# Two attention passes interleaved pair by pair, and key tiles transposed in a score bank

## The chip, the cores and the metric

The kernel runs on one core of one Trainium2 chip. The metric is the device time of one execution in microseconds (us); the median of three runs stands against the median of the changed kernel. Engines are named as the profile names them: PE is TensorE's matmul stream and PEld its weight loads, DVE is VectorE, ACT is ScalarE, POOL is GpSimd, SP is the engine that issues most DMAs.

## The reference, cut to what matters

A perceiver block: cross attention of 256 latent rows on 4096 context rows, then a random-feature attention, then a mixture of experts. The change touches only the first.

```python
xn = layernorm(x, ln_x_g, ln_x_b)              # 4096 context rows of 256
ln = layernorm(latents, ln_l_g, ln_l_b)        # 256 latent rows
q = (ln @ Wq).reshape(b, m, h, d).transpose(0, 2, 1, 3)   # 16 heads of 64
kv = jnp.concatenate([xn @ Wkv, ln @ Wkv], axis=1)
qn = rmsnorm(q, qn_g) * scale
kn = rmsnorm(k, kn_g)
sim = jnp.einsum('bhid,bhjd->bhij', qn, kn)
attn = softmax(sim)
out = einsum(attn, v)                          # then out @ Wout + bout
```

(In the kernel, x of this block is the context and the latents are the model's 256 rows; both kinds of rows are keys, so there are 4352 of them.)

## The kernel before, in words

**Tiles, units, passes.** The 4352 key rows are 34 tiles of 128 rows (`NT`), taken two at a time as 17 units (`NU`). The 16 heads are done in 4 passes (`NPASS`) of 4 heads. A step n is one tile in one pass, so there are 136 steps; the program is written in pairs m of two steps, 68 in all, 17 of each pass. Steps run pass by pass: pair 0 to 16 is pass 0, 17 to 33 is pass 1, and so on.

**Preparing a unit**, once, in pass 0: VectorE takes row statistics (`statistics`, L618 and L625), GpSimd the root (`root_of`, L810 and L815), ScalarE and VectorE subtract the mean and scale a tile each (`center`, L482 and L639), TensorE transposes four 128x128 blocks (`transpose_z`, L345) into a PSUM bank, ScalarE applies the gain (`gain`, L491) and rounds to fp32r (L495), VectorE keeps the rounding rest (`rest`, L645) in `xn`. Products of fp32 numbers are taken as three fp32r products of first parts and rests.

**A step**: TensorE projects a tile on keys and values (`project`, L168, 6 matmuls of 512 columns into `kv_ps`); ScalarE squares the keys (`square`, L516) and keeps the values (`keep_v`, L523); VectorE sums (`mean_square`, L689), GpSimd takes the root (`root`, L796), VectorE scales (`scale_k`, L667, tile `kn`); TensorE transposes (`transpose_k`, L372), ScalarE and VectorE split the result (`keep_kt`, L530, and `kt_rest`, L693); TensorE takes the scores (`scores`, L386, two banks for each parity of n); ScalarE takes the exponents (`weights`, L538), VectorE adds them up (`add_weights`, L683), TensorE weights the values (`weight_v`, L399, into `o_ps` of the pass's parity).

**Order.** Each engine runs its own hand-written loop over m, in order, and waits on semaphores. In pair m with e = 2m, TensorE does project(e+2), project(e+3), transpose_k(e), transpose_k(e+1), the query work if it is due, transpose_z(m+3), weight_v(e-2), weight_v(e-1), scores(e), scores(e+1). ScalarE does weights(e-2), weights(e-1), square(e+2), keep_kt(e), keep_kt(e+1), keep_v(e+2), square(e+3), keep_v(e+3), gain(m+3), center(m+4). VectorE does add_weights of e-2 and e-1, with rest(m+2) behind the first, mean_square(e+2), kt_rest(e), kt_rest(e+1), statistics(m+4), the last add_weights, scale_k(e+2), mean_square(e+3), center(m+4), scale_k(e+3). `project(n)` waits for kn and v of step n-2, since `kv_ps` has two banks.

**Between passes.** Queries of pass t are made over five pairs around `query_pair(t, 0)`: `queries_hi` on ScalarE (L501), `queries_lo` on GpSimd (L819), `project_q` on TensorE, `square_q`, `mean_square_q` (L649), `root_q` (L823), `scale_q` (L653), `transpose_q`, and at stage 2 `keep_qt` (ScalarE L510) and `qt_rest` (VectorE L659). The pass's weights are split by `weights_hi` (ScalarE L548) and `weights_lo` (GpSimd L801, one instruction of 1024 columns). For pass 1 stage 0 is pair 14 and the weights fall in pairs 11 and 12.

Of the kernel before, what the change touches and what calls it, by code (L numbers as in the profile page):

```python
# [178 lines left out]
def attention(nc, sem, a, x_res, ident, ones, neg_half, fw, ew):  # L179
# [4 lines left out]

    V_RING = 6
    P_RING = 4
    with ExitStack() as ctx:
# [58 lines left out]

        def exists(n):
            return 0 <= n < STEPS

# [3 lines left out]
        def zt_ps(k):  # L253

            return o_ps[1][:, k, :]
# [9 lines left out]
        def ended(m):  # L265

            g = (m + 1) // NU - 1
            return g if 0 <= g < NPASS and (g + 1) * NU - 1 == m else None

        def query_pair(t, stage):  # L270

            return (NU - 3 if t == 1 else (t - 1) * NU + 9) + stage

        @block.sync
        def _(sp):
# [18 lines left out]
            sp.dma_start(bout[:], a["L0_xattn_bout"].partition_broadcast(P)).then_inc(bout_in, 16)  # L294
            for g in range(4, NG + 1):
# [17 lines left out]
            for g in range(1, NPASS):  # L313
                sp.wait_ge(wq_lo, g)
                load_queries(g)
                sp.wait_ge(w_lo, g)
                load_weights(g)
                if g >= 2:
                    sp.wait_ge(y_done, g - 1)
                    load_wout(g - 1)  # L320
# [4 lines left out]
        def _(pe):  # L325
            def project(n):
                g, t, b = n // NT, n % NT, n % 2
                if t == 0:
                    pe.wait_ge(w_lo, g + 1)
# [18 lines left out]
            def project_q(t):  # L348
                if t == 0:
                    pe.wait_ge(xn_lo, 1)  # L350
                elif t == 1:
                    pe.wait_ge(affine_done, NU)
                else:
                    pe.wait_ge(y_added, t - 1)
# [20 lines left out]
            def scores(n):  # L375
                g, b = n // NT, n % 2
                pe.wait_ge(kt_lo, n - n % 2 + 2)
                if n % NT == 0:
                    pe.wait_ge(qt_lo, g + 1)
                if n >= 2:  # L380
                    pe.wait_ge(exp_done, 2 * (n - 1))
                for j in range(2):
                    for t, (s, m) in enumerate(((0, 0), (0, 1), (1, 0))):
                        for c in range(2):
                            half = slice(c * DH, (c + 1) * DH)
                            last = nc.tensor.matmul(s_ps[b][c][:, j, :], kt[b][half, s, j * P:(j + 1) * P],  # L386
                                                    q_parts[g % 2][half, j, m, :], start=t == 0, stop=t == 2)
                            if j == 1 and t == 2:
                                last.then_inc(s_done, 1)

            def weight_v(n):
                g, t = n // NT, n % NT
# [11 lines left out]
            def totals(g):  # L404
                pe.wait_ge(sum_done, 2 * (g + 1) * NT)
# [24 lines left out]
            for m in range(STEPS // 2 + 1):  # L430
# [14 lines left out]
                if m + 3 < NU:  # L445
                    transpose_z(m + 3)
# [18 lines left out]
        def _(act):  # L465
# [53 lines left out]
            def keep_v(n):  # L519
                if n >= V_RING:  # L520
                    act.wait_ge(pv_done, n - V_RING + 1)
                t = n % NT
# [17 lines left out]
            def keep_sums(g):  # L540
                act.wait_ge(pv_done, (g + 1) * NT)
# [27 lines left out]
            for m in range(STEPS // 2 + 1):  # L569
# [18 lines left out]
                if m + 3 < NU:  # L588
# [904 lines left out]
```

## Time and profile before

| | us |
|---|---|
| median of three runs | 704.05 (703.61 to 705.65) |
| time of the profiled execution | 703.4 |
| its span in the trace | 701.7 |
| PE busy in the span | 660.5 (94%) |
| DVE busy | 499.3 (71%) |
| ACT busy | 417.2 (59%) |
| POOL busy | 236.7 (34%) |

The attention takes the trace from the start to about 540 us, of which 36.2 to 540 is the regular loop. Busy time of PE holds overlaps of one matmul with the next, so the length of a pair is best read from the distance between two starts of the same work, for which `weight_v` (L399) is taken below.

### The profile page before, as it was taken

What the parts mean: (1) busy time and instruction counts of PE and PEld (TensorE: products, weight loads), DVE (VectorE), ACT (ScalarE), POOL (GpSimd) and SP (SyncE); (2) the same over time, 40 slices, a digit from 0 to 9 for tenths busy, and PEclk for the clock granted to TensorE, in tenths of its full rate; (3) what the DMA queues carried; (4) which work ended last, traced back from release to release, by engine and by line L of the source; (5) the groups of instructions that cost most, each with busy time, mean ns of one, the idle gap of its engine ahead of it and who ended that gap; (6) DMA issues with size and microseconds to landing.
All of it is one profiled execution on the core that took longest, in us unless ns stands there. A gap on an engine that the chain in (4) does not pass through costs nothing. (4 is left out here: it accounts for less than half of the span.)

```text
span 701.7 us, 14395 instructions
## 1 busy us (share of the span) xinstructions
PE 660.5 (94%) x5152; PEld 526.8 (75%) x5152; DVE 499.3 (71%) x977; ACT 417.2 (59%) x878; POOL 236.7 (34%) x219
## 2 busy tenths in 40 slices
PE   1899999899999999999999999999998997899997
PEld 0777776677677777777777777777776886899997
DVE  2798898866867677687768767767676636867573
ACT  3687888656556666665666666566663313565650
POOL 3544434532233242222334332232220023355640
PEclk9999999999999999999999999999999989999999
DMA  5111460100000000000000000000002104256500
GB/s 161 36 56 32 123 182 1 46 1 2 1 16 16 2 31 1 2 1 16 1 2 1 1 2 1 16 2 1 1 2 68 53 1 164 78 196 218 166 19 16
DMA packets 26131, 30.50 MB, mean 43 GB/s; under 512 B 4169, under 2 KB 23762, under 8 KB 26066
## 3 DMA queue, kind: packets, MB, share of 16 engines
q1 hardware_dynamic: 23410, 28.79, 12.9%
q10 hardware_dynamic: 2656, 0.86, 0.5%
q8 instruction: 39, 0.64, 0.4%
q14 instruction: 26, 0.21, 0.1%
HBM read 29.38 MB, written 0.26 MB: 42 GB/s over the span
## 5 line engine op out<-in xcount | busy, mean ns | idle before, releaser
L796 POOL TENSOR_TENSOR k_rms<-k_ss,neg_half 128x4 f32<-128x4 f32 x136 | 137.1, 1008 | 312.6 <-DVE k_ss L689 312.6
L538 ACT ACTIVATE probs<-s_ps,minus_bound 128x512 f32<-128x512 f32 x272 | 164.6, 688 | 90.2 <-PE s_ps L386 90.2
L168 PE MATMUL kv_ps<-w_quad,xn 128*128 128x512 f32 x816 | 211.0, 405 | 1.6 <-issue 1.5
L683 DVE SCALAR_TENSOR_TENSOR probs_sum<-probs,tile_mask,probs_sum 128x512 f32<-128x512 f32 x264 | 192.4, 765 | 5.2 <-ACT probs L538 4.8
L168 PEld LDWEIGHTS kv_ps<-w_quad,xn 128*128 128x128 f32 x816 | 147.3, 188 | 45.0 <-issue 6.4
L399 PE MATMUL o_ps<-probs,v 128*64 128x256 f32 x1088 | 132.6, 385 | 0.8 <-ACT probs L538 0.7
L386 PEld LDWEIGHTS s_ps<-q_parts,kt 64*128 64x128 f32 x1632 | 101.1, 185 | 36.0 <-issue 19.6
L386 PE MATMUL s_ps<-q_parts,kt 64*128 64x256 f32 x1632 | 114.9, 287 | 9.2 <-DVE kt L693 9.2
L667 DVE SCALAR_TENSOR_TENSOR kn<-k_rms,kv_ps 128x256 f32<-128x256 f32 x136 | 56.7, 417 | 67.5 <-POOL k_rms L796 67.0
L399 PEld LDWEIGHTS o_ps<-probs,v 128*64 128x64 f32 x1088 | 72.0, 136 | 41.9 <-issue 10.7
L530 ACT ACTIVATE kt<-s_ps 128x256 fp32r<-128x256 f32 x136 | 44.9, 383 | 63.9 <-PE s_ps L372 63.6
L693 DVE TENSOR_TENSOR kt<-s_ps,kt 128x256 fp32r<-128x256 f32 x136 | 51.0, 416 | 33.0 <-ACT kt L530 33.0
L523 ACT ACTIVATE v<-kv_ps,tile_mask 128x256 f32<-128x256 f32 x136 | 66.4, 488 | 0.0
L689 DVE TENSOR_REDUCE k_ss<-k_sq 128x4 f32<-128x256 f32 x136 | 55.9, 411 | 1.8 <-ACT k_sq L516 1.7
L516 ACT ACTIVATE k_sq<-kv_ps 128x256 f32<-128x256 f32 x136 | 54.2, 399 | 1.8 <-PE kv_ps L168 1.8
L372 PE MATMUL s_ps<-ident,kn 128*128 128x128 f32 x272 | 41.2, 273 | 0.6 <-ACT probs L538 0.6
L372 PEld LDWEIGHTS s_ps<-ident,kn 128*128 128x128 f32 x272 | 33.7, 140 | 10.4 <-issue 1.0
L1392 DVE CAST e_act_p<-e_act_f 128x1024 fp32r<-128x1024 f32 x18 | 17.7, 985 | 26.3 <-PE e_y_ps L1300 25.6
L1348 ACT ACTIVATE e_act_f<-e_h_ps,e_b_now 128x256 f32<-128x256 f32 x72 | 27.7, 486 | 5.6 <-DVE e_act_p L1394 3.5
L1246 POOL TENSOR_TENSOR w_first<-w_raw,w_first 128x2048 fp32r<-128x2048 f32 x4 | 21.6, 5402 | 23.5 <-ACT w_first L1332 23.5
L1246 POOL TENSOR_TENSOR e_w_second<-w_raw,e_w_second 128x2048 fp32r<-128x2048 f32 x4 | 21.5, 5364 | 23.6 <-ACT e_w_second L1332 19.6
L168 PE MATMUL e_h_ps<-e_zp,w_first 128*128 128x256 f32 x240 | 29.0, 280 | 0.4 <-DVE e_zp L1416 0.4
(185 smaller groups left out, 666.7 us busy)
## 6 DMA issues: line engine op xcount, KB each, us to landing
w_raw<-in_ffn_W SPq DMA_DIRECT2D x18, 1024.0 KB, 5.2
rows<-in_ctx SPq DMA_DIRECT2D x8, 512.0 KB, 3.9
w_raw<-in_L_xattn_Wkv SPq DMA_DIRECT2D x6, 256.0 KB, 3.1
wout<-in_L_xattn_Wout SPq DMA_DIRECT2D x4, 256.0 KB, 2.7
wq_raw<-in_L_xattn_Wq SPq DMA_DIRECT2D x3, 256.0 KB, 3.3
w_raw<-in_L_xattn_Wkv ACTq DMA_DIRECT2D x2, 256.0 KB, 6.7
x_res<-in_x SPq DMA_DIRECT2D x1, 256.0 KB, 3.6
wq_raw<-in_L_xattn_Wq ACTq DMA_DIRECT2D x1, 256.0 KB, 4.1
```

The source lines that it names most:

```text
L168: last = nc.tensor.matmul(out, stationary(k, s), moving(k, m), start=n == 0, stop=n == len(terms) - 1)
L372: last = nc.tensor.transpose(kt_ps(n)[:, j * P:(j + 1) * P], kn[n % 2][:, j].rearrange("p c d -> p (c d)"), ident[:])
L386: last = nc.tensor.matmul(s_ps[b][c][:, j, :], kt[b][half, s, j * P:(j + 1) * P], q_parts[g % 2][half, j, m, :], start=t == 0, stop=t == 2)
L399: last = nc.tensor.matmul(o_ps[g % 2][c * DH:(c + 1) * DH, j, :], v[n % V_RING][:, j, c, :], probs[n % P_RING][:, j, c, :], start=t == 0 a ...
L516: nc.scalar.activation(k_sq[n % 2][:].rearrange("p j c d -> p (j c d)"), kv_ps[n % 2][:, 0, :], ACT.Square, scale=DH ** -0.5).then_inc(sq_ ...
L523: nc.scalar.activation(v[n % V_RING][:].rearrange("p j c d -> p (j c d)"), kv_ps[n % 2][:, 1, :], ACT.Copy, scale=tile_mask[:, t:t + 1]).t ...
L538: nc.scalar.activation(probs[n % P_RING][:, :, c, :], s_ps[n % 2][c][:], ACT.Exp, bias=minus_bound[:]).then_inc(exp_done, 1)
L667: nc.vector.scalar_tensor_tensor(kn[n % 2][:], k_rms[n % 2][:].unsqueeze(3).to_broadcast([P, 2, 2, DH]), 1.0 / RMS_FLOOR, kv_ps[n % 2][:, ...
L683: nc.vector.scalar_tensor_tensor(total, probs[n % P_RING][:, :, c, :], seen, total, ALU.mult, ALU.add).then_inc(sum_done, 1)
L689: nc.vector.reduce_sum(k_ss[n % 2][:], k_sq[n % 2][:], AX_X).then_inc(ss_done, 1)
L693: nc.vector.tensor_tensor(kt[n % 2][:, 1, :], kt_ps(n), kt[n % 2][:, 0, :].bitcast(F32), ALU.subtract).then_inc(kt_lo, 1)
L796: nc.gpsimd.tensor_tensor(k_rms[n % 2][:].rearrange("p i c -> p (i c)"), k_ss[n % 2][:].rearrange("p i c -> p (i c)"), neg_half[:, 0:4], A ...
```

## The change

The order of pairs is now a list, `plan`: four pairs of pass 0, then one of pass 1 before every two of pass 0, until pass 0 is through (plan positions 4, 7, 10, 13, 16, 19 and 22 are pass 1), then the rest of pass 1, and passes 2 and 3 as before. Pass 0 ends at position 23, pass 1 at 33. `unit_of` gives the pair in which a unit is transposed: pairs 0, 2, 3, 5, 6, 8, 9, 11, 12, 14, 15, 17, 18 and 20 for units 3 to 16; its statistics and center stand one pair ahead, its rest one pair behind. Since both `o_ps` banks are in use, a unit is transposed in `s_ps[1][0]`, a score bank: the transposes wait for the exponents of step e-1, half 0, and scores(e+1) waits for `gain`. `gain` moves ahead of keep_v(e+2). Pass 1's queries and weights are now due at the very start (stage 0 is pair 2, `weights_hi` pair 0, `weights_lo` pairs 1 and 2), those of pass 2 at pairs 31 and 26 to 28. `weights_lo` is two instructions of 512 columns, a pair apart.

```diff
+        ahead, plan = 4, []
+        for u in range(NU):
+            if u >= ahead and (u - ahead) % 2 == 0:
+                plan.append((1, (u - ahead) // 2))
+            plan.append((0, u))
+        taken = sum(g for g, _ in plan)
+        plan += [(1, u) for u in range(taken, NU)] + [(g, u) for g in range(2, NPASS) for u in range(NU)]
+        place = {step: m for m, step in enumerate(plan)}
+        unit_of = {place[0, u] - 3: u for u in range(3, NU)}
...
-            return o_ps[1][:, k, :]
+            return s_ps[1][0][:, k, :]
...
-            return (NU - 3 if t == 1 else (t - 1) * NU + 9) + stage
+            return (2, 2 * NU - 3, 2 * NU + 9)[t - 1] + stage
+        def weights_pair(g):
+            return (0, place[0, NU - 1] + 3, 2 * NU + 11)[g - 1]
...
+                if u >= 4:
+                    pe.wait_ge(exp_done, 2 * (2 * (place[0, u] - 3) - 1) + 1)
...
+                if b and n // 2 in unit_of:
+                    pe.wait_ge(affine_done, unit_of[n // 2] + 1)
...
-                if m + 3 < NU:
-                    transpose_z(m + 3)
+                if m in unit_of:
+                    transpose_z(unit_of[m])
...
+                if m in unit_of:
+                    gain(unit_of[m])
                 if exists(e + 2):
                     keep_v(e + 2)
                     square(e + 3)
                     keep_v(e + 3)
-                if m + 3 < NU:
-                    gain(m + 3)
...
-                    if m == query_pair(t, -3):
+                    if m == query_pair(t, -2):
                         queries_hi(t)
...
+                if m - 1 in unit_of:
+                    rest(unit_of[m - 1])
...
-                    if m == query_pair(t, -2):
+                    if m == query_pair(t, -1):
                         queries_lo(t)
...
-                if m % NU == NU - 5 and m // NU < NPASS - 1:
-                    weights_lo(m // NU + 1)
+                    for k in range(KD):
+                        if m == weights_pair(t) + 1 + k:
+                            weights_lo(t, k)
```

VectorE, from the scaled keys at the end of pair 2 to the key parts of pair 3. `q_ss` and `qn` are the query work, `xn` is rest(4) here and rest(5) before, `kt` the key parts for which the scores of pair 3 wait. Before:

```order
L667 SCALAR_TENSOR_TENSOR kn<-k_rms,kv_ps 128x256
L779 TENSOR_TENSOR x_res<-x_res,bout 128x512
L683 SCALAR_TENSOR_TENSOR probs_sum<-probs,tile_mask,probs_sum 128x2x256
L645 TENSOR_TENSOR xn<-affine,xn 128x2x2x128
L683 SCALAR_TENSOR_TENSOR probs_sum<-probs,tile_mask,probs_sum 128x2x256 x2
L689 TENSOR_REDUCE k_ss<-k_sq 128x4
L693 TENSOR_TENSOR kt<-s_ps,kt 128x256 x2
```

and after:

```order
L696 SCALAR_TENSOR_TENSOR kn<-k_rms,kv_ps 128x256
L678 TENSOR_REDUCE q_ss<-q_sq 128x8
L810 TENSOR_TENSOR x_res<-x_res,bout 128x512
L682 SCALAR_TENSOR_TENSOR qn<-q_rms,o_ps 128x512
L712 SCALAR_TENSOR_TENSOR probs_sum<-probs,tile_mask,probs_sum 128x2x256
L674 TENSOR_TENSOR xn<-affine,xn 128x2x2x128
L712 SCALAR_TENSOR_TENSOR probs_sum<-probs,tile_mask,probs_sum 128x2x256 x2
L718 TENSOR_REDUCE k_ss<-k_sq 128x4
L722 TENSOR_TENSOR kt<-s_ps,kt 128x256 x2
```

Two query instructions now stand between the scaled keys and the first sum of exponents.

GpSimd, after the changed loop has begun, pairs 1 and 2 (`wq`, `w_quad` are pass 1's query and key-value weights, `q_rms` its queries' root); before, pairs 1 and 2 hold only the two roots and the unit's root:

```order
L850 TENSOR_TENSOR wq<-wq_raw,wq 128x2x256
L832 TENSOR_TENSOR w_quad<-w_raw,w_quad 128x512
L827 TENSOR_TENSOR k_rms<-k_ss,neg_half 128x4
L841 TENSOR_SCALAR var_eps<-mean_var 128x2
L846 TENSOR_TENSOR rstd<-var_eps,neg_half 128x2
L827 TENSOR_TENSOR k_rms<-k_ss,neg_half 128x4
L854 TENSOR_TENSOR q_rms<-q_ss,neg_half 128x8
L832 TENSOR_TENSOR w_quad<-w_raw,w_quad 128x512
```

ScalarE in pair 0, from the key parts to the first exponents. Before:

```order
L530 ACTIVATE kt<-s_ps 128x256 x2
L523 ACTIVATE v<-kv_ps,tile_mask 128x256
L516 ACTIVATE k_sq<-kv_ps 128x256
L523 ACTIVATE v<-kv_ps,tile_mask 128x256
L491 ACTIVATE affine<-o_ps,gains 128x256 x2
L495 ACTIVATE xn<-affine 128x2x2x128
L482 ACTIVATE z<-rows,mean_off,rstd 128x256
L538 ACTIVATE probs<-s_ps,minus_bound 128x2x256 x4
```

and after:

```order
L559 ACTIVATE kt<-s_ps 128x256 x2
L520 ACTIVATE affine<-s_ps,gains 128x256 x2
L524 ACTIVATE xn<-affine 128x2x2x128
L552 ACTIVATE v<-kv_ps,tile_mask 128x256
L545 ACTIVATE k_sq<-kv_ps 128x256
L552 ACTIVATE v<-kv_ps,tile_mask 128x256
L530 ACTIVATE wq<-wq_raw 128x2x256
L577 ACTIVATE w_quad<-w_raw 128x2x512
L567 ACTIVATE probs<-s_ps,minus_bound 128x2x256 x4
```

The gain moved ahead of the kept values and the square, and the weights' first parts stand where the center of the next unit stood.

## Rows read from the trace of the kernel before

**Rows 1.** Page, the span in 40 slices: busy tenths of PE

```profile
PE   1899999899999999999999999999998997899997
```

**Rows 2.** Windows from weight_v to weight_v: stretch, length, busy PE, PEld, DVE, ACT, POOL

```profile
213.61:220.56 6.95, 6.95 (x57) 5.22 (x56) 5.50 (x10) 4.36 (x11) 2.66 (x3) 1.00 0.11 37
220.56:228.91 8.35, 8.35 (x69) 6.67 (x68) 5.92 (x13) 5.78 (x15) 3.03 (x3) 1.00 0.01 2
36.23:43.61 7.38, 7.38 (x62) 5.66 (x61) 6.59 (x17) 6.40 (x16) 3.33 (x4) 1.00 0.03 10
50.97:59.05 8.08, 7.64 (x61) 5.58 (x61) 7.30 (x18) 6.40 (x16) 3.33 (x4) 1.00 0.00 1
59.05:66.61 7.56, 7.56 (x61) 5.56 (x60) 6.77 (x18) 6.39 (x15) 3.33 (x4) 1.00 0.23 63
111.99:119.96 7.97, 7.80 (x61) 5.49 (x60) 5.72 (x17) 6.80 (x14) 3.33 (x4) 1.00 0.00 0
119.96:128.60 8.64, 7.71 (x62) 5.57 (x61) 7.86 (x17) 7.35 (x19) 6.33 (x6) 1.00 0.04 8
128.60:139.02 10.42, 8.42 (x70) 6.67 (x69) 9.29 (x18) 6.88 (x17) 3.71 (x4) 1.00 0.22 71
153.31:161.23 7.92, 7.00 (x58) 5.22 (x57) 6.80 (x14) 4.36 (x11) 2.02 (x2) 1.00 0.00 0
```

**Rows 3.** Timeline of a pair with a unit: start, length, engine, line, work

```profile
83.62 1.69 PE L386 MATMUL s_ps<-q_parts,kt 64*128 64x256 f32 x24
...
86.35 0.42 DVE L667 SCALAR_TENSOR_TENSOR kn<-k_rms,kv_ps 128x256 f32<-128x256 f32 x1 [0.50 <-POOL k_rms L796]
...
86.84 1.23 PEld L168 LDWEIGHTS kv_ps<-w_quad,xn 128*128 128x128 f32 x6 [0.37 <-issue]
```

**Rows 4.** Timeline of a pair without a unit, pass 1

```profile
215.48 1.71 PE L386 MATMUL s_ps<-q_parts,kt 64*128 64x256 f32 x24
...
217.10 0.42 DVE L667 SCALAR_TENSOR_TENSOR kn<-k_rms,kv_ps 128x256 f32<-128x256 f32 x1 [1.12 <-POOL k_rms L796]
```

**Rows 5.** Timeline: sums and rests of VectorE beside GpSimd's weight rests

```profile
126.80 2.83 POOL L801 TENSOR_TENSOR w_quad<-w_raw,w_quad 128x1024 fp32r<-128x1024 f32 x1
...
127.32 2.85 DVE L645 TENSOR_TENSOR xn<-affine,xn 128x512 fp32r<-128x512 f32 x1
...
132.54 1.69 PE L386 MATMUL s_ps<-q_parts,kt 64*128 64x256 f32 x24 [2.00 <-DVE kt L693]
...
248.80 2.07 DVE L683 SCALAR_TENSOR_TENSOR probs_sum<-probs,tile_mask,probs_sum 128x512 f32<-128x512 f32 x3
...
254.96 3.87 DVE L683 SCALAR_TENSOR_TENSOR probs_sum<-probs,tile_mask,probs_sum 128x512 f32<-128x512 f32 x3
```

**Rows 6.** Timeline of pairs 0 and 1: ScalarE's gain and exponents, second projection

```profile
30.56 1.05 ACT L491 ACTIVATE affine<-o_ps,gains 128x256 f32<-128x256 f32 x2
...
31.64 0.63 ACT L495 ACTIVATE xn<-affine 128x512 fp32r<-128x512 f32 x1
...
33.27 0.42 DVE L667 SCALAR_TENSOR_TENSOR kn<-k_rms,kv_ps 128x256 f32<-128x256 f32 x1 [0.49 <-POOL k_rms L796]
...
33.79 1.64 PE L168 MATMUL kv_ps<-w_quad,xn 128*128 128x512 f32 x6 [0.24 <-issue]
```

**Rows 7.** Timeline of pass 2's query work: scores, sum, scaled queries, scores two pairs later

```profile
230.79 1.69 PE L386 MATMUL s_ps<-q_parts,kt 64*128 64x256 f32 x24
231.34 0.68 DVE L649 TENSOR_REDUCE q_ss<-q_sq 128x8 f32<-128x512 f32 x1
...
233.77 0.69 DVE L653 SCALAR_TENSOR_TENSOR qn<-q_rms,o_ps 128x512 f32<-128x512 f32 x1 [1.75 <-POOL q_rms L823]
...
246.07 1.70 PE L386 MATMUL s_ps<-q_parts,kt 64*128 64x256 f32 x24 [0.92 <-DVE kt L693]
```

**Rows 8.** One line each: GpSimd's query weight rest, VectorE's rest, min/median/max ns

```profile
L819 POOL TENSOR_TENSOR wq<-wq_raw,wq x4: 1282/1296/1449, 16.4 to 341.7; 128x512 fp32r<-128x512 f32 x4
L645 DVE TENSOR_TENSOR xn<-affine,xn x17: 677/685/2855, 15.9 to 135.9; 128x512 fp32r<-128x512 f32 x17
```

More of the change, by code:

```diff
@@ L245, in attention, with step, last_step @@
         block = ctx.enter_context(nc.Block())
+        ahead, plan = 4, []
[7 more added lines that the diff above has]
+        unit_of = {place[0, u] - 3: u for u in range(3, NU)}
         def exists(n):
             return 0 <= n < STEPS
+        def step(n):
+            g, u = plan[n // 2]
+            return g, 2 * u + n % 2
+        def last_step(g):
+            return 2 * place[g, NU - 1] + 1
         def source(u):
@@ L312, in _ @@
                 sp.dma_start(fw.proj_bd[DHP * h:DHP * (h + 1), h, :], a["L0_attn_proj"]).then_inc(fw.proj_in, 16)
-            for g in range(1, NPASS):
+            for g in range(2, NPASS):
                 sp.wait_ge(wq_lo, g)
                 load_queries(g)
-                sp.wait_ge(w_lo, g)
+                sp.wait_ge(w_lo, KD * g)
                 load_weights(g)
-                if g >= 2:
-                    sp.wait_ge(y_done, g - 1)
-                    load_wout(g - 1)
+                sp.wait_ge(y_done, g - 1)
+                load_wout(g - 1)
             sp.wait_ge(y_done, NPASS - 1)
@@ L326, in project @@
             def project(n):
-                g, t, b = n // NT, n % NT, n % 2
+                (g, t), b = step(n), n % 2
                 if t == 0:
-                    pe.wait_ge(w_lo, g + 1)
+                    pe.wait_ge(w_lo, KD * (g + 1))
                 if g == 0:
@@ L375, in scores @@
             def scores(n):
-                g, b = n // NT, n % 2
+                (g, t), b = step(n), n % 2
                 pe.wait_ge(kt_lo, n - n % 2 + 2)
-                if n % NT == 0:
+                if t == 0:
                     pe.wait_ge(qt_lo, g + 1)
@@ L386, in scores @@
                             last = nc.tensor.matmul(s_ps[b][c][:, j, :], kt[b][half, s, j * P:(j + 1) * P],
-                                                    q_parts[g % 2][half, j, m, :], start=t == 0, stop=t == 2)
-                            if j == 1 and t == 2:
+                                                    q_parts[g % 2][half, j, m, :], start=term == 0, stop=term == 2)
+                            if j == 1 and term == 2:
                                 last.then_inc(s_done, 1)
             def weight_v(n):
-                g, t = n // NT, n % NT
+                g, t = step(n)
                 if t == 0:
@@ L596, in _ @@
                         square_q(t)
-                if m % NU == NU - 6 and m // NU < NPASS - 1:
-                    weights_hi(m // NU + 1)
+                    if m == weights_pair(t):
+                        weights_hi(t)
             keep_sums(NPASS - 1)
@@ L671, in add_weights @@
             def add_weights(n, c):
-                g, t = n // NT, n % NT
+                g, t = step(n)
                 dve.wait_ge(exp_done, 2 * n + 1 + c)
@@ L749, in _ @@
                     add_weights(e - 2, 0)
-                if m + 2 < NU:
-                    rest(m + 2)
+                if m == 0:
+                    rest(2)
+                if m - 1 in unit_of:
+                    rest(unit_of[m - 1])
                 if exists(e - 2):
@@ L759, in _ @@
                         kt_rest(n)
-                if m + 4 < NU:
-                    statistics(m + 4)
+                if m + 1 in unit_of:
+                    statistics(unit_of[m + 1])
                 if exists(e - 2):
@@ L832, in _ @@
             root_of(1)
-            weights_lo(0)
+            for k in range(KD):
+                weights_lo(0, k)
             queries_lo(0)
@@ L856, in _ @@
                         root_q(t)
-                if m % NU == NU - 5 and m // NU < NPASS - 1:
-                    weights_lo(m // NU + 1)
+                    for k in range(KD):
+                        if m == weights_pair(t) + 1 + k:
+                            weights_lo(t, k)
                 if m == 10:
```

39 lines of the change are left out of this document (21 added, 18 removed).

## The prediction
> **What bounds the kernel now.** I read the page's slices first: from the second slice to the end of the attention PE stands at 9 tenths and at 8 in one slice [rows 1]. A busy PE hides waits of some tenths, so next come windows cut from one weight_v to the next. A pair of pass 1 takes 6.95 us, the first row of [rows 2]; PE is the limit there, since almost all pairs of three passes have that length. The same pair with a query projection takes 8.35, so that work is 1.40. The second pair of pass 0, with a unit, takes 7.38 (36.23 to 43.61), so the four transposes of a unit cost 0.43 of TensorE. Any length beyond 6.95, plus 0.43 with a unit, plus 1.40 with queries, is a wait. The change gives TensorE the same matmuls in another order, so the only thing that can move is the sum of these waits, in the first 24 to 36 pairs.
>
> **The waits of before that the change touches** [rows 2]:
> - Seven ordinary pairs of pass 0 between 59 and 112 us have 7.56, not 7.38: 0.18 each, 1.3 in all. The cause is in the timeline: with a unit, the second scaled key (kn) starts 2.73 us after the scores of its pair begin (86.35 against 83.62) and the second projection of the next pair starts only behind it, at 3.22, with 0.37 idle in front [rows 3]; without a unit kn starts at 1.62 (217.10 against 215.48) [rows 4] and nothing waits. The chain behind a unit is 1.1 us longer, and its slack was some 0.9.
> - 8.08 at 50.97: the same with an addition of `bout` on VectorE, 0.7.
> - 7.97, 8.64 and 10.42 at 112 to 139, where pass 1's weights and queries are made beside units: 0.59 + 1.26 + (10.42 - 6.95 - 1.40 =) 2.07 = 3.9. The largest part is one row: rest (L645), 0.68 as a rule [rows 8], took 2.85 while GpSimd took its weight rest, and the scores then waited 2.00 for kt [rows 5].
> - 7.92 at 153.31, stage 2 of pass 1's queries: 0.97.
> In all 1.3 + 0.7 + 3.9 + 1.0 = **6.9 us** of waits. All of it is gone or moved; TensorE's own work is not less. That is the most that the change could give.
>
> **What comes in their place.** The query and weight work of pass 1 now lies in pairs 0 to 4, which also prepare units, with an empty pipeline behind them. S(m) is the start of the scores of pair m.
> - *Pair 0.* ScalarE's gain (1.05 + 0.63 [rows 6]) now stands ahead of the second square, which comes about 2.0 later. VectorE and GpSimd hid part of that: kn of step 3 goes from 33.27 to about 34.0, and the projection behind it from 33.79 to 34.5: **0.7**.
> - *Pair 1.* Statistics without transposes: kn ends about 3.3 after S(1), where TensorE could project at about 3.0: **0.35**. Behind it GpSimd takes wq and the first half of w_quad, 1.3 each (the 512 columns of [rows 8]).
> - *Pair 2.* The two GpSimd rests run while VectorE wants to add exponents. What that costs is in the trace: three sums took 2.07 alone and 3.87 while GpSimd took 1024 columns [rows 5]. I take 1.3 to 2 us; it uses up most of the 1.40 that the query projection gives the other engines. What is left of it is a late kn, **0.3**. That VectorE is less ahead is what matters next.
> - *Pair 3.* In pass 2 the scaled queries (qn) start 2.98 after the scores (233.77 against 230.79), the sum before them at 0.55 [rows 7]. Here kn is 2.6 later against the scores (a unit with its statistics 1.1, GpSimd's rests about 1.5), so q_ss begins near 3.2 and qn, 2.43 behind it as in [rows 7], near 5.6; it ends at 6.3. TensorE's transpose_q, due at 5.0, waits **1.2** for it. Then VectorE has still to do, before kt: one sum that waits out the second w_quad half on GpSimd (0.6), three sums (2.0), rest 0.6, k_ss 0.35 and kt 0.75, which ends near 10.6. The scores could start at 9.1. A further **1.6**.
> - *Pair 4.* Stage 2: `qt_rest` waits for ScalarE behind the exponents, which cost 0.92 in pass 2 [rows 7]; here rest(5) (0.6) stands in the same row, ahead of kt: **1.6**.
> - *Pair 5.* VectorE has no slack left from pair 4, and statistics follow at once. kn is 0.7 later than in an ordinary unit pair: 0.18 + 0.7, **0.85**.
> In all 6.6 us; the same counted over the whole stretch from S(0) to S(5) gave 6.4, which I take.
> - *Later units, pairs 6 to 20.* Where transposes and statistics fall in one pair (8, 11, 14, 17), VectorE has no rest to take there and is 0.6 earlier: no wait. In pairs with transposes alone kn ends about 2.7 after the scores, 0.3 before TensorE wants it: none. In pairs with statistics alone (7, 10, 13, 16, 19) TensorE lacks the 0.43 of cover, and kn is 0.1 later than in [rows 3]: 0.3 each, **1.5**.
> - *The new waits.* Scores(e+1) waits for the gain. Behind the transposes TensorE has weight_v, 1.87 (213.61 in [rows 2] to 215.48 in [rows 4]), and scores(e), half of 1.69; the gain needs 1.05 [rows 6] of these 2.7, so it costs nothing, and 1.6 us of lateness of ScalarE are covered. The transposes wait for the third of four exponents, and weight_v right behind them needs the second and the fourth anyway: nothing.
> - *The rest.* Prologue 0.2 (GpSimd's two halves are 2.6 where one was 2.4, and VectorE's rest waits for them); the first half of pass 2's weights beside the normalisation of pass 0, 0.1. Loads of pass 1 are issued from 16 us on and needed from 33: hidden. Query stages of passes 2 and 3 stay as they are.
> Sum: 6.4 + 1.5 + 0.3 = 8.2 of waits for 6.9, **1.3 us more**. The profiled execution would go from 703.4 to 704.7; the median of before lies 0.65 above its profiled execution, so the forecast is 704.05 + 1.3 = **705.3**. Against the early chain stands no row of the same place, so I bound it: if GpSimd's rests fit in gaps and qn is as early as in [rows 7], pairs 0 to 5 cost 2.5, and the whole comes to 4.3 - 6.9 = -2.6; if each step adds, 9 us and +3.9.
>
> A rule beside this. The rows show a VectorE instruction with both inputs in SBUF lengthened by as much as GpSimd's overlaps it (2.85 for 0.68, 3.87 for 2.07) [rows 5]. The Trainium skill, in "SBUF — State Buffer", section "Who interferes with whom", says that such an instruction and a GpSimd instruction that reads SBUF exclude each other, and that the one issued later is blocked for the whole instruction. By that rule the `bout` addition in pair 2 also holds back GpSimd's root of the queries, by up to 0.6, and the sum would be 1.9 and the time 705.9; I left it out, as no row shows a root held back by it.
>
> **Rivals.**
> - *Faster: the early pairs are absorbed.* For: VectorE has 1.1 to 1.4 idle in a pair without a unit, and two of pairs 0 to 5 have none to transpose; in pass 2 the query stages 0 and 1 cost nothing. Against: the 3.87 row and that rest and queries meet in pairs 3 and 4. Pairs 0 to 5 at 2.5 and the statistics pairs at 0 to 1.5: 704.05 - 2.6 to -4.1, about **700.7**. Chance 0.2.
> - *Slower: gain ahead of keep_v makes ScalarE's chain the limit in every unit pair.* The second square of a pair comes 1.68 later; VectorE's sum of squares is 0.6 later in a pair with transposes alone than in [rows 4], and kn has 0.9 to spare there. It decides once the lateness passes 0.9. At 0.3 beyond that, in 14 unit pairs, 4.2 more: 704.05 + 1.3 + 4.2 = **709.5**. Chance 0.12.
> - *Slower: the early chain at its upper bound*, 9 us for pairs 0 to 5: 704.05 + 3.9 = **708**. Chance 0.16.
> - *The plan does not do what it says*: the even spread brings no pair under 7.38, since TensorE was the limit. This is no case of its own; it is what the sum rests on.
>
> **How the numbers follow.** Forecast case 0.52, at 705.3, itself 703.5 to 707. About 0.3% is what a measurement of this kernel can tell from no change: 702.0 to 706.1. The forecast case lies mostly within (0.43), a little above (0.09); the faster rival lies below 702 with 0.17 and within with 0.03; both slower rivals are above, 0.28. So faster 0.17, the same 0.46, slower 0.37. The range takes the forecast, most of the faster rival and the upper bound of the early chain: 701.0 to 708.5.
>
> **What would show it.** From weight_v to weight_v: 6.95 for plain pairs, 7.38 for pairs with transposes from pair 6 on, 7.2 to 7.3 in pairs behind statistics alone; the 10.42 gone; two long pairs at plan positions 3 and 4 with kt as what the scores wait for; a DVE rest and sums lengthened beside w_quad at 41 to 54 us. Wrong would be: waits of the scores for `affine` (ScalarE) on PE, waits in each unit pair, or a first stretch to pair 5 that is no more than 3 us longer than TensorE's work.

## The result, and the profile after

| | before | after |
|---|---|---|
| time, median of 7 runs each | 704.06 us (703.27 to 705.86) | 707.75 us (706.92 to 708.18) |
| profiled execution | 703.4 us | 706.92 us |
| its span | 701.7 us | 705.1 us |
| first to last weight_v (windows) | 491.13 us | 495.90 us |

The changed kernel is slower: the ratio is 1.0046, with an interval of 1.0036 to 1.0056. That is 3.7 us where +1.3 was forecast, and above the bound of 0.3%. The likeliest case had been "the same"; the time lies inside the range.

The page of after, first its busy times, then TensorE's two rows of slices:

```profile
PE 660.0 (94%) x5152; PEld 526.9 (75%) x5152; DVE 498.5 (71%) x977; ACT 418.5 (59%) x878; POOL 238.4 (34%) x223
...
PE   1878999999999999999999999999998998899997
...
PEclk9998999999999999999999999999999999999999
```

Against [rows 1] the third and fourth slice of PE (35.3 to 70.5 us) have fallen from 9 to 7 and 8, and the eighth (123 to 141 us), where the pair of 10.42 us was, has risen from 8 to 9. In the fourth slice the granted clock is lower too.

The same windows as in [rows 2], from weight_v to weight_v (stretch, length, busy PE, PEld, DVE, ACT, POOL, granted clock, DMA share, GB/s). The window of pair m begins with the weight_v of pair m and holds the scores of pair m and then the projections and transposes of pair m+1; the first five are pairs 1 to 5 of the plan, the last two are later ones:

```profile
36.63:45.84 9.21, 9.03 (x73) 7.00 (x72) 8.42 (x18) 5.59 (x14) 6.28 (x6) 1.00 0.19 57
45.84:60.88 15.04, 9.99 (x65) 7.72 (x65) 9.66 (x23) 7.09 (x15) 7.58 (x7) 0.77 0.00 1
60.88:67.81 6.93, 6.93 (x57) 5.21 (x56) 2.94 (x7) 6.04 (x13) 1.01 (x1) 1.00 0.00 0
67.81:77.65 9.84, 7.71 (x61) 5.58 (x61) 8.78 (x22) 5.29 (x13) 3.36 (x5) 1.00 0.15 51
77.65:85.00 7.35, 7.35 (x61) 5.64 (x60) 6.62 (x17) 6.49 (x15) 3.33 (x4) 1.00 0.02 7
...
91.92:99.54 7.62, 7.58 (x61) 5.57 (x60) 6.83 (x19) 5.28 (x13) 3.34 (x5) 1.00 0.23 62
99.54:106.91 7.37, 7.37 (x61) 5.66 (x60) 6.66 (x17) 6.50 (x15) 3.34 (x4) 1.00 0.03 10
```

The count of matmuls tells what is in a window: 57 is a plain pair (6.95), 61 holds four transposes as well (+0.43), 65 holds eight (+0.86), 73 holds a query projection and four transposes (+1.83). What is beyond that is waiting: 9.21 - 8.78 = 0.43; 15.04 - 7.81 = **7.23**; 6.93 nothing; 9.84 - 7.38 = 2.46; then nothing. One window stands out, 45.84 to 60.88, and its clock (0.77) says that part of its excess is no wait at all. It is the window of pair 2; what the prediction counts as its pair 3, from the scores of pair 2 to those of pair 3, lies in it and in the start of the next.

The timeline of that window, with two rows of pair 0 ahead of it and one of pair 4 behind it (start, length, engine, line, work, and in brackets the idle time before it and what ended it):

```profile
30.66 1.69 PE L415 MATMUL s_ps<-q_parts,kt 64*128 64x256 f32 x24 [0.61 <-DVE kt L722]
...
34.62 1.64 PE L168 MATMUL kv_ps<-w_quad,xn 128*128 128x512 f32 x6 [0.23 <-issue]
...
47.72 1.68 PE L415 MATMUL s_ps<-q_parts,kt 64*128 64x256 f32 x24
...
50.39 0.68 DVE L678 TENSOR_REDUCE q_ss<-q_sq 128x8 f32<-128x512 f32 x1
...
50.99 0.68 DVE L810 TENSOR_TENSOR x_res<-x_res,bout 128x512 f32<-128x512 f32 x1
...
51.15 2.01 POOL L854 TENSOR_TENSOR q_rms<-q_ss,neg_half 128x8 f32<-128x8 f32 x1 [1.13 <-DVE q_ss L678]
...
53.13 1.26 POOL L832 TENSOR_TENSOR w_quad<-w_raw,w_quad 128x512 fp32r<-128x512 f32 x1
...
54.45 5.19 PE L168 MATMUL kv_ps<-w_quad,xn 128*128 128x512 f32 x12 [5.05 <-POOL w_quad L832]
...
64.38 3.07 PE L168 MATMUL kv_ps<-w_quad,xn 128*128 128x512 f32 x12
...
71.27 1.69 PE L415 MATMUL s_ps<-q_parts,kt 64*128 64x256 f32 x24 [1.51 <-DVE kt L722]
```

After the scores of pair 2 (47.72) TensorE is to project for pair 4 of the plan, the first of pass 1. That projection is the first to read pass 1's `w_quad`, and the second half of this tile is the last work of GpSimd's own pair 2. GpSimd's sequence at that point is q_rms, then the weight rest; q_rms waits for `q_ss`, the sum that VectorE gets to at 50.39. So the rest lands at 54.39, and TensorE, whose scores ended at 49.40, has stood for 5.05 us. Then it pays again: its clock fell during the wait, and the two projections take 5.19 where the same 12 matmuls take 3.07 in the next pair. The window over those first matmuls gives the clock (0.50, the 1.2 GHz level); the trace has it at that level from 52.34 to 59.17:

```profile
54.45:57.00 2.55, 2.55 (x6) 2.07 (x7) 2.42 (x4) 0.00 (x0) 0.00 (x0) 0.50 0.02 6
```

Of the view of TensorE's waits over the span, the two lines that bear on the loop:

```profile
PE s_ps L415 <- DVE kt L722: 7.5, 10, 1.5
...
PE kv_ps L168 <- POOL w_quad L832: 5.0, 1, 5.0
```

The whole loop (first to last weight_v) and the stretch behind it up to the first transposes of the expert stage, of before and then of after:

```profile
36.23:527.36 491.13, 480.17 (x3869) 360.95 (x3869) 370.20 (x773) 324.06 (x729) 166.15 (x169) 1.00 0.07 19
527.36:585.12 57.76, 53.98 (x295) 44.86 (x295) 30.83 (x54) 16.01 (x19) 7.22 (x6) 0.94 0.13 40
```

```profile
36.63:532.53 495.90, 481.89 (x3873) 363.25 (x3872) 371.50 (x781) 325.12 (x730) 168.51 (x174) 0.99 0.06 18
532.53:588.71 56.18, 52.40 (x294) 43.27 (x295) 30.82 (x54) 16.02 (x19) 7.16 (x6) 0.97 0.13 40
```

The loop is 4.8 us longer. The stretch behind it is 1.6 shorter, with code that the change does not touch: TensorE's clock stood at 1.2 GHz for 3.41 us there, where it had been 6.83 us before. The prologue adds 0.4 (the first scores begin at 30.66 for 30.26), pair 0 costs another 0.43, and the first weight_v comes only 0.4 later all the same, because the four transposes of unit 4 (0.43) have moved behind it. So 4.8 + 0.4 stands at the last weight_v, and 4.8 + 0.4 - 1.6, with 0.2 less in the last stage, is the 3.4 us between the spans. So the loop's window is the measure for everything below; totals carry 1.6 us or more that come and go with the clock of the later stages. (The stretches at the lower clock are taken from the trace's own clock records; a window gives their sum, as (1 - 0.97) of 56.18, twice, is 3.4.)

### The profile page after: what moved, and what is told of

Read it like the earlier page. It is cut to its first block and busy times, and to the rows that moved or that the text cites. A ratio compares the mean times of both kernels' runs of the same rounds, so it can differ in the third digit from the quotient of the medians.

```text
span 705.1 us, 14413 instructions
## 1 busy us (share of the span) xinstructions
PE 660.0 (94%) x5152; PEld 526.9 (75%) x5152; DVE 498.5 (71%) x977; ACT 418.5 (59%) x878; POOL 238.4 (34%) x223
## 5 line engine op out<-in xcount | busy, mean ns | idle before, releaser
L168 PEld LDWEIGHTS kv_ps<-w_quad,xn 128*128 128x128 f32 x816 | 149.1, 190 | 50.2 <-issue 5.8
L1279 POOL TENSOR_TENSOR e_w_second<-w_raw,e_w_second 128x2048 fp32r<-128x2048 f32 x4 | 21.4, 5362 | 23.5 <-ACT e_w_second L1365 19.6
```

Of the source, the lines that this page charges most:

```text
L168: last = nc.tensor.matmul(out, stationary(k, s), moving(k, m), start=n == 0, stop=n == len(terms) - 1)
```

## The experiments

Three questions were open: how much of the loss is the wait for the weights (e1, e2); whether the unit's new place or order costs anything alone (e4); and whether the interleave has a gain of its own, or whether its parts in the old order do the same (e3, e5, e6, e7, e8, e9). Ratios are times against the kernel before.

### e1: both weight halves in one pair

```diff
-                        if m == weights_pair(t) + 1 + k:
+                        if m == weights_pair(t) + 1 + (k if t > 1 else 0):
                             weights_lo(t, k)
```

> Edit on the changed kernel: both halves of pass 1's w_quad rest run on GpSimd in pair 1, none in pair 2 behind the queries' root. Theory (first projection of pass 1 waits for the second half, 5.05 us, and TensorE's clock falls to its lower level behind that wait, which costs another 2.2): the wait for w_quad and the low clock are gone; in their place come the waits for the scaled queries and for kt that the prediction counted, 2 to 3 us in pair 3. Attention 7.2 - 2.8 = 4.4 us shorter, total 703 to 704. Rival (the wait only hides an equally late chain on VectorE): pair 3 still takes over 13 us, total 707 or more.

Measured: 705.4 us, ratio 1.0017 (1.0006 to 1.0027). Its loop, and the window that was 15.04:

```profile
37.59:529.37 491.78, 480.31 (x3873) 361.57 (x3872) 371.97 (x781) 324.94 (x730) 168.92 (x174) 1.00 0.06 19
```

```profile
46.82:57.02 10.20, 8.34 (x66) 6.00 (x65) 7.82 (x19) 6.87 (x15) 5.55 (x6) 1.00 0.00 0
```

What is left to wait for there, from its timeline:

```profile
50.57 1.64 PE L168 MATMUL kv_ps<-w_quad,xn 128*128 128x512 f32 x6 [0.19 <-issue]
...
52.51 1.67 PE L168 MATMUL kv_ps<-w_quad,xn 128*128 128x512 f32 x6 [0.29 <-DVE kn L696]
...
53.13 2.01 POOL L854 TENSOR_TENSOR q_rms<-q_ss,neg_half 128x8 f32<-128x8 f32 x1 [1.13 <-DVE q_ss L678]
...
55.99 0.66 PE L389 MATMUL o_ps<-ident,qn 128*128 128x128 f32 x4 [1.38 <-DVE qn L682]
...
59.57 1.69 PE L415 MATMUL s_ps<-q_parts,kt 64*128 64x256 f32 x24 [0.61 <-DVE kt L722]
```

The window is 4.84 shorter, 0.67 comes back in the next one (7.60 for 6.93), and the loop is 4.1 shorter, as expected. The loop is now 0.65 above that of before. With the weights out of the way TensorE waits for a late kn (the projections start late and with a gap, about 0.8 together by the distances between starts), then for qn (1.38 idle, 1.5 by the starts), and then for kt (0.61 idle, 0.65 in the next window): those are the three waits that the prediction had put here. The edit also takes the second half's hold on VectorE out of this pair, so it does not leave the rest exactly as in the changed kernel. The total came out 1.4 above the 704 of the expectation. Its profiled execution shows where: by the trace's clock records TensorE's clock rose at 24.36 us instead of 21.62, so its first projections took 4.46 instead of 3.20 and the loop began 1 us later (ahead of these records the clock row reads 1.00, but the 12 matmuls of the query projection take 2.90 there in both traces and 1.66 in the loop), and the stretch behind the loop was back at 57.78.

### e2: something for TensorE to do while it waits

Twenty matmuls of the identity are run ahead of the wait for the weight half. They leave the real work as it is; nothing reads what they write. The profile shows each as two records (x40).

```diff
             def project(n):
                 (g, t), b = step(n), n % 2
+                if t == 0 and g == 1:
+                    pe.wait_ge(kn_done, n - 1)
+                    pe.wait_ge(v_kept, n - 1)
+                    keep_busy(nc, kv_ps[b][:, 0, 0:P], ident[:], ident[:], 20)
```

> Edit on the changed kernel: 20 matmuls of the identity (results are never read) stand on TensorE ahead of the wait for w_quad, so that the wait stays but TensorE is busy in most of it. Theory: the granted clock stays at its upper level from 52 to 59 us, the two projections behind the wait take 3.1 us in place of 5.2, pair 3 goes from 15.0 to about 12.8, and the total falls by about 2 us unless later stages give it back. Rival (the 5.2 us of these projections have another cause, such as reads of w_quad beside GpSimd): pair 3 stays at 15.0 and the time stays at 707.7.

Measured: 706.46 us, ratio 1.0031 (1.0018 to 1.0044). Its loop, and the window:

```profile
36.78:530.66 493.88, 484.48 (x3913) 366.19 (x3912) 371.54 (x781) 325.14 (x730) 168.47 (x174) 1.00 0.06 19
```

```profile
46.02:58.92 12.90, 12.54 (x106) 10.64 (x105) 9.57 (x23) 7.09 (x15) 7.59 (x7) 1.00 0.00 1
```

```profile
49.52 4.73 PE L176 MATMUL kv_ps<-ident 128*128 128x128 f32 x40
...
54.61 3.06 PE L168 MATMUL kv_ps<-w_quad,xn 128*128 128x512 f32 x12 [0.36 <-POOL w_quad L836]
```

The weights come at the same time as in after (the projections start at 54.61 against 54.45), but the clock stays at 1.00 and they take 3.06 instead of 5.19. The window is 2.14 shorter and the loop 2.0. So of the 4.2 us that e1 won, half was the wait and half was the clock that the wait had cost. The total fell only 1.3: behind the loop 1.6 us came back (57.82 against 56.18).

### e4: the unit in a score bank and the gain ahead of keep_v, in the order of before

```diff
-            return o_ps[1][:, k, :]
+            return s_ps[1][0][:, k, :]
...
+                if u >= 4:
+                    pe.wait_ge(exp_done, 2 * (2 * (u - 3) - 1) + 1)
...
+                if b and n // 2 + 3 < NU:
+                    pe.wait_ge(affine_done, n // 2 + 4)
...
+                if m + 3 < NU:
+                    gain(m + 3)
```

(and `gain(m + 3)` taken out where it stood before).

> Edit on the kernel before: only the transposes of units move to the score bank, with their two waits, and gain moves ahead of keep_v; pass order, queries and weights stay. Theory: the new waits and the moved gain cost nothing in unit pairs: 7.56 us a pair or a little less, total 703.5 to 704.5. Rival (gain ahead of keep_v makes ScalarE's chain the limit): 7.8 to 7.9 us in the 14 unit pairs, total 707.5 to 708.5.

Measured: 705.43 us, ratio 1.0019 (1.0010 to 1.0028). The loop, and an ordinary pair with a unit:

```profile
37.66:528.87 491.21, 480.37 (x3870) 360.98 (x3869) 370.31 (x773) 325.26 (x729) 166.13 (x169) 1.00 0.06 19
```

```profile
68.05:75.61 7.56, 7.56 (x61) 5.57 (x60) 6.78 (x18) 6.49 (x15) 3.33 (x4) 1.00 0.03 11
```

The loop is that of before to 0.1 us, and the unit pair is 7.56, as in [rows 2]. The two new waits of TensorE cost nothing in the loop, and ScalarE's earlier gain does not make it late. The rival of 709.5, in which it would, falls. The total missed its expectation by 0.9 at the least (705.43 for 703.5 to 704.5), and what the parts cost lies ahead of the loop, which begins 1.4 later: from the start of pair 0's projections to the first weight_v 11.28 us against 10.48, so 0.8, the price of the gain in pair 0; the other 0.6 is again a clock that rose later (22.99 against 21.54 us, first projections 3.92 against 3.33).

### e5: the old order, pass 1's weights two pairs later

In the kernel before, pass 1's weight rest (pair 12) stands beside the last units and the rest of the query weights. It can be moved out of their way in the order of before too, with two numbers: ScalarE's part to pair 13 and GpSimd's to pair 14.

```diff
-                if m % NU == NU - 6 and m // NU < NPASS - 1:
+                if m in (NU - 4, 2 * NU - 6, 3 * NU - 6):
                     weights_hi(m // NU + 1)
...
-                if m % NU == NU - 5 and m // NU < NPASS - 1:
+                if m in (NU - 3, 2 * NU - 5, 3 * NU - 5):
                     weights_lo(m // NU + 1)
```

> Edit on the kernel before: pass 1's weights are split two pairs later (ScalarE in pair 13, GpSimd in pair 14), behind the last units; no interleaving. Theory (the 3.9 us of waits in pairs 11 to 13 come from queries, weights and units meeting on ScalarE and GpSimd, above all the rest that waited out GpSimd's w_quad): 2.5 to 3.5 us faster, total 700.5 to 701.5. Rival (late weights hold up the start of pass 1, or the scaled queries wait instead): within 1 us of 704.

Measured: 704.02 us (700.0 to 704.84), ratio 0.9979 (0.9962 to 0.9996). The loop, the windows that were 8.64 and 10.42 in [rows 2], and one of the pair two further on:

```profile
36.75:525.88 489.13, 479.88 (x3869) 360.99 (x3869) 369.54 (x773) 323.95 (x729) 165.77 (x169) 1.00 0.07 19
```

```profile
120.11:128.19 8.08, 7.64 (x62) 5.58 (x61) 7.29 (x18) 6.79 (x17) 4.57 (x5) 1.00 0.07 24
128.19:136.53 8.34, 8.34 (x70) 6.66 (x69) 7.21 (x17) 7.72 (x18) 2.78 (x3) 1.00 0.04 12
...
143.90:151.86 7.96, 7.01 (x58) 5.22 (x57) 5.51 (x12) 4.51 (x11) 2.02 (x2) 1.00 0.20 67
```

The 10.42 is now 8.34, where TensorE has no idle time at all, and 8.64 is 8.08. The pair ahead of them is 7.58 for 7.97. One new wait came: the last window has 1.04 more than before (7.96 for 6.92), 0.95 of it idle before the scores, for kt. The three sums that VectorE takes ahead of kt are 3.59 long there, beside GpSimd's weight rest, where they were 2.07 in before. The loop is 2.0 shorter than before and 6.8 shorter than after. The expectation of 2.5 to 3.5 us was missed: 3.0 were gained in three pairs, and 1.0 came back. The median shows less of it (704.02, where before had 704.24 beside it), since its executions lie apart: 700.0 to 700.4 at a granted clock of 0.995, 703.9 to 704.8 at 0.988. The largest of the waits that the interleave spreads is gone without an interleave.

### e3: the halves alone

In the order of before, GpSimd's weight rest is taken in two halves, one in each of two pairs; nothing else is moved.

```diff
-            def weights_lo(g):
+            def weights_lo(g, k):
...
-                if m % NU == NU - 5 and m // NU < NPASS - 1:
-                    weights_lo(m // NU + 1)
+                for k in range(KD):
+                    if m % NU == NU - 5 + k and m // NU < NPASS - 1:
+                        weights_lo(m // NU + 1, k)
```

> Edit on the kernel before: only the w_quad rest in two halves on GpSimd, a pair apart (pairs 12 and 13 for pass 1). Theory: each half shuts out VectorE's two-input work for 1.3 us in place of 2.8 at once; pairs 12 and 13 go from 8.64 and 10.42 to about 8.0 and 9.2, the loop is 1.5 to 2 us shorter, total 702 to 703. Rival (the total of the lock counts, not its length at once): loop as before within 0.5 us.

Measured: 702.19 us, ratio 0.9978 (0.9966 to 0.9990). The loop, the window that was 10.42, and VectorE's rest that had been 2.85 in [rows 5]:

```profile
37.58:527.96 490.38, 480.30 (x3869) 360.98 (x3868) 369.24 (x773) 324.03 (x729) 166.48 (x172) 1.00 0.07 19
```

```profile
129.91:139.26 9.35, 8.43 (x70) 6.68 (x69) 8.23 (x16) 6.89 (x17) 3.28 (x3) 1.00 0.21 71
```

```profile
128.65 1.77 DVE L645 TENSOR_TENSOR xn<-affine,xn 128x512 fp32r<-128x512 f32 x1
```

The rest is held for one half only, 1.77 for 2.85, and the window of the queries gains 1.07 (10.42 to 9.35). The one before it gains nothing (8.64, 8.62), and the one two further on has 0.3 more. The loop gains 0.75, less than the 1.5 to 2 expected: the weight rests are still in the pairs of the last units, and halving them doesn't take them out of there as e5 does. The total is better than the loop by the clock behind the loop (3.4 us at the lower level, 56.15 for 57.76): this ratio must not be read against that of e5.

### e6: both, and `bout` in pair 20

The edits of e3 with ScalarE's part in pair 12 and the halves in pairs 13 and 14, and the addition of `bout` moved:

```diff
-                if m == 2:
+                if m == 20:
```

> Edit on the kernel before: pass 1's weights on ScalarE in pair 12 and their rest in two halves on GpSimd in pairs 13 and 14; the addition of bout moves from pair 2 to pair 20. Theory: of the 6.9 us of waits that the prediction listed, the 0.7 of bout and 2.5 to 3.5 of the 3.9 in pairs 11 to 13 go; from the first to the last weight_v 491.1 becomes 487 to 488, total 700 to 701.5, as far as the low-clock stretches of the later stages do not move. Rival (each delay only moves): loop no shorter than the 489.1 of the run with late weights.

Measured: 703.35 us, ratio 0.9979 (0.9963 to 0.9996). The loop, the pair after 20, and the stretch behind the loop:

```profile
36.81:525.90 489.09, 479.71 (x3869) 361.41 (x3868) 367.99 (x773) 323.31 (x729) 166.05 (x172) 1.00 0.06 19
```

```profile
187.94:198.36 10.42, 8.72 (x65) 6.73 (x64) 7.63 (x16) 4.35 (x11) 3.02 (x3) 1.00 0.01 2
...
525.90:585.31 59.41, 55.64 (x294) 46.39 (x295) 30.84 (x54) 16.01 (x19) 7.15 (x6) 0.91 0.13 38
```

The loop is that of e5. The pair that `bout` left is 7.46 (8.08 before), 0.62 better, but the pair between 187.94 and 198.36 is 10.42 where it had been 9.69: there the normalisation of pass 0's output wants VectorE too, and 0.73 is lost again. The 487 to 488 expected for the loop was missed, and the rival, a loop no shorter than 489.1, held: the wait had only moved. The last row has the lower clock for 10.24 us, and is 1.65 longer than that of before.

### e7: e1, and `bout` in pair 24

```diff
-                if m == 2:
+                if m == 24:
```

(beside the edit of e1).

> Edit on the changed kernel: w_quad's rest wholly in pair 1, and bout's addition moved from pair 2 to pair 24. Theory (the addition held back GpSimd's root of the queries, 2.01 us in place of 1.64): the root takes 1.64 again and pair 3 is 0.3 to 0.4 shorter than the 10.2 without this move. Rival (the root is long because of its own data or the sum before it): root 2.0, pair 3 at 10.2.

Measured: 704.96 us, ratio 1.0010 (0.9999 to 1.0021). The loop, and the window that was 10.20 in e1, with GpSimd's root of the queries in it:

```profile
36.54:527.93 491.39, 480.39 (x3874) 361.60 (x3873) 372.15 (x781) 324.92 (x730) 168.36 (x174) 1.00 0.06 19
```

```profile
45.77:55.52 9.75, 8.33 (x66) 6.00 (x65) 7.21 (x18) 6.87 (x15) 5.17 (x6) 1.00 0.01 2
```

```profile
52.08 1.64 POOL L854 TENSOR_TENSOR q_rms<-q_ss,neg_half 128x8 f32<-128x8 f32 x1 [1.13 <-DVE q_ss L678]
```

The root takes 1.64 without the addition beside it, and 2.01 with it (after and e1), 0.37 more; the window is 0.45 shorter and the loop 0.4.

### e8: the interleave begins four pairs later

If an empty pipeline were the cause of the waits, the same steps some pairs later would be free.

```diff
-        ahead, plan = 4, []
+        ahead, plan = 8, []
...
-            return (2, 2 * NU - 3, 2 * NU + 9)[t - 1] + stage
+            return (6, 2 * NU - 3, 2 * NU + 9)[t - 1] + stage
...
-            return (0, place[0, NU - 1] + 3, 2 * NU + 11)[g - 1]
+            return (4, place[0, NU - 1] + 3, 2 * NU + 11)[g - 1]
```

(with the edit of e1).

> Edit on the changed kernel: pass 1 begins at plan position 8 in place of 4, its queries are made around pair 6 and its weights in pairs 4 and 5 (w_quad's rest wholly in pair 5). Theory (what costs is that queries, weights and units meet, not that the pipeline has just begun): the pairs from weight_v 5 to 9 hold 4.5 to 6 us of waits, as the pairs 1 to 5 do when w_quad is early (0.4 + 2.4 + 0.7 + 2.5), and the loop is 491.5 to 492.5. Rival (the empty pipeline was the cost): under 3 us of waits there, loop 489 to 490.

Measured: 705.58 us, ratio 1.0011 (0.9993 to 1.0028). The loop, and three of the four windows:

```profile
37.59:529.00 491.41, 479.76 (x3869) 361.18 (x3869) 369.86 (x773) 325.10 (x729) 166.85 (x172) 1.00 0.06 18
```

```profile
67.34:76.81 9.47, 9.07 (x73) 7.00 (x72) 8.69 (x17) 5.40 (x13) 7.75 (x7) 1.00 0.17 56
76.81:86.56 9.75, 8.33 (x66) 6.00 (x65) 7.22 (x18) 6.87 (x15) 5.17 (x6) 1.00 0.00 1
...
94.15:103.99 9.84, 7.72 (x62) 5.58 (x61) 8.78 (x22) 5.29 (x13) 3.35 (x5) 1.00 0.17 49
```

Less TensorE's own work these windows wait 0.69, 1.94 and 2.46, and the one between them (7.60, a plain pair) 0.65: 5.7 in all. In e1 the same four wait 0.45 + 2.39 + 0.67 + 2.46 = 6.0 from the second pair of the plan on. The 0.3 between them is `bout`, which no longer stands there. So the empty pipeline is not the cause. What is left is that weights, queries and a unit's statistics want VectorE and GpSimd in the same pairs; e5, which takes the weights out of the units' pairs in the old order, speaks for it, but no run does so in the interleaved one.

### e9: e5, and `bout` in pair 24

```diff
-                if m == 2:
+                if m == 24:
```

(beside the edits of e5).

> Edit on the kernel before: pass 1's weights late (ScalarE in pair 13, GpSimd in pair 14), and bout's addition moved from pair 2 to pair 24, where no unit, query or normalisation stands. Theory (an addition on VectorE costs only where a unit or a normalisation leaves no slack; in pair 20 it cost the next projection out 0.74): pair 3 is 7.5 in place of 8.1, pair 24 stays at 6.95, the loop from first to last weight_v is 488.4 to 488.6. Rival (any added 0.68 us on VectorE is paid somewhere): loop 489.1 as with late weights alone.

Measured: 701.76 us (699.57 to 703.35), ratio 0.9960 (0.9945 to 0.9974). The loop, and the pair that was 8.08:

```profile
37.02:525.59 488.57, 479.72 (x3870) 361.09 (x3869) 369.53 (x773) 323.94 (x729) 165.79 (x169) 1.00 0.06 19
```

```profile
51.74:59.21 7.47, 7.47 (x62) 5.58 (x61) 6.68 (x18) 6.40 (x16) 3.33 (x4) 1.00 0.01 4
```

The loop is 2.6 below that of before, as expected, and the kernel is 2.8 us faster than before and 6.0 faster than the changed one, by its median: three numbers changed in the old order. Executions at the same granted clock say the same: at 0.992 it takes 701.5 to 701.8 where before takes 703.3 to 704.1, at 0.988 703.0 to 703.4 for 705.7 to 706.2.

## Why the prediction was right or wrong

**What bounds the kernel: right.** TensorE was the limit, and the time went by the sum of its waits. The windows less TensorE's own work, known from their matmul counts, account for the change of the loop to 0.1 us (below). One reading was off: in [rows 1] the second slice is an 8 too, so the nines begin at the third; nothing hangs on it.

**Pairs 0, 1, 2: right, but for the split.** Pair 0 was put at 0.7; kn was to go to about 34.0 and came at 34.10, and the projection behind it to 34.5 and came at 34.62. But 0.40 of that lateness was there when pair 0's scores began, so pair 0 itself cost 0.43 and the prologue 0.40 where 0.2 was forecast; together 0.83 for 0.9. In e4, with a unit's statistics and center still in pair 0, the gain costs 0.8. Pair 1 was put at 0.35 and is 0.43. For pair 2 a late kn was put at 0.3; in the changed kernel the wait for the weights covers it, in e1 it is about 0.8.

**Pair 3: the step that failed.** The prediction went from "TensorE's transpose_q, due at 5.0, waits 1.2 for it" to "A further 1.6" for kt, 2.8 in all, 3.1 with pair 2. The windows of pairs 2 and 3 measured 7.23. The "due at 5.0" assumes that TensorE's projections ahead of transpose_q can run. It had the second w_quad half on GpSimd in this very pair, but only as a load on VectorE ("one sum that waits out the second w_quad half on GpSimd"). It did not ask who waits for the half itself: the projection, and it stands ahead of the transposes on TensorE. Nor did it lay out GpSimd's queue, in which the half stands behind q_rms, and q_rms behind a VectorE sum. e1 takes this wait away, and with it the half's hold on VectorE in this pair, and leaves 2.39 + 0.67 = 3.1 in this window and the next, the size forecast. The split is not the one forecast: kn 0.8 for 0.3, qn 1.5 for 1.2, kt 0.65 for 1.6, so that the sum agrees this well is in part luck. What was missing is a wait of 5.05 that overlapped with them, worth 2.1 beyond them, and its sequel, the clock, worth 2.1 more (e2: 2.0 in the loop).

**Pairs 4 and 5: right.** Put at 1.6 and 0.85, 2.45 together; the window that holds both measured 2.46. Of that 1.6 lies ahead of the scores of pair 4 (1.51 of it idle, for kt), and the rest in the projections behind them, as forecast; the next window (7.35) has none.

**Later units: right.** No waits in pairs with transposes (7.37), 0.25 in the pairs that follow statistics alone (7.62), in five windows 1.3 where 1.5 had been put. The forecast length of those, 7.2 to 7.3, left out that the next unit's transposes fall into the same window; the wait was what it said.

**The new waits: right.** No wait for a gain or for the exponents in the loop of after, and e4 shows it alone: 491.21 against 491.13. TensorE's one wait for `affine` (1.30, at 15.56 us) lies ahead of the first scores and is 1.30 in the kernel before too.

**The root held back: a real cost.** The prediction left out up to 0.6 that q_rms might lose to the `bout` addition. The rows show 2.01 beside the addition and 1.64 without it (e7), 0.37; the loop of e7 is 0.4 shorter. It was smaller than its bound, and smaller than the 0.52 in which the two rows overlap. By the Trainium skill, "SBUF — State Buffer", "Who interferes with whom", a VectorE instruction with two SBUF inputs contends with a GpSimd instruction that reads SBUF, and the order of issue decides who waits. Here the addition began at 50.99 and the root at 51.15; that the root, the later one, is lengthened agrees, while a root blocked for the whole rest of the addition would have lost 0.52. What the prediction left out here should have been a term of its sum.

**The waits removed: right in size, but cheaper to remove.** 6.9 of waits were to go. The loop's balance bears this out: 10.1 in pairs 1 to 4 and 1.3 later is 11.4, and the unit transposed inside the loop instead of ahead of it is 0.43 of work; less 6.9 that is 4.9, and the loop measured 4.8 more. What the prediction did not ask is which part needed the interleave. e5 and e9 remove 2.0 and 2.6 of them in the old order.

**The sum.** Added waits of 8.2 were forecast. What came is 0.4 in the prologue, 0.43 in pair 0, 10.1 in pairs 1 to 4 and 1.3 later, 12.2 in all, of which the missed wait and its clock are 4.2; without these it is 8.0. Less 6.9 that is 5.3, and the last weight_v stands 5.2 later (532.53 for 527.36). Then the profiled execution got 1.6 back behind the loop and 0.2 in the last stage, so that 5.2 became 3.4 in the span. Without the 1.6 the total would have stood near 709, above the range; as far as any run shows, that it lies inside is luck. The 709 is worked out, not measured. The prediction assumed without saying so that the stages behind the loop keep their length; their clock doesn't let them.

**The rivals.** The absorbed early pairs (700.7) didn't happen: even in e1 pairs 1 to 4 wait 6.0. The ScalarE chain (709.5) is refuted by e4. The early chain at its upper bound had the total (708) but not the mechanism: its 9 us for pairs 0 to 5 were passed (10.6), and not because each step added; one wait that it didn't name did it.

What stays open: why the stretch behind the loop has its clock at the lower level for 3.4 us in one kernel, 6.8 in another and 10.2 in a third. No run set out to steer it. Open too is how e1's kn, qn and kt would have measured with the second half's hold on VectorE still in the pair.

## What to carry to other kernels

When work is moved earlier, write out for each tile not only what its making costs the other engines but who reads it first, and what stands ahead of its making in the maker's queue; here that one line would have shown the 5 us wait, and here the wait cost the clock on top. Try single due times in the old order before a reorder: here three of them took 2.6 us off the loop, where the interleave added 4.8. And measure a loop between two starts of the same work, from first to last, since here the stage behind it, the same code in all kernels, took from 56.15 to 59.41 us.

## What the runs showed of the hardware

- In a mid-loop wait of TensorE of 5.05 us (49.40 to 54.45) the granted clock fell to 0.50 (1.2 GHz) and stayed there from 52.34 to 59.17: 12 matmuls took 5.19 instead of 3.07. With identity matmuls in the wait (4.73 us of them) the clock stayed at 1.00 and they took 3.06. The longest single wait elsewhere in a loop, 2.00 us for kt in before, had no such sequel (its window shows 1.00).
- The stretch from the last weight_v to the expert stage, the same code in all kernels, took 56.15 to 56.18 with 3.4 us at the lower clock, 57.76 to 57.95 with 6.8, and 59.41 with 10.2, so about 1.6 more each time. Together with a clock that rose between 21.4 and 24.4 us at the start (first projections 3.20 or 4.46), this fits how far the executions of one kernel differ, more than most edits here are worth: e5 took 700.0 to 700.4 in the executions with a mean granted clock of 0.995, 702.4 to 702.8 at 0.990, and 703.9 to 704.8 at 0.988.
- GpSimd's root over 8 columns takes 1.64 alone and 2.01 when a VectorE addition of two SBUF tiles has begun 0.16 before it. VectorE's rest takes 0.68 alone [rows 8], 1.77 beside a half weight rest on GpSimd (e3) and 2.85 beside the whole one [rows 5].
